# Gate and up projections by seven Strassen products, over pairs of inner chunks

## What is computed

```python
x = layernorm(x + attention(x))                  # 4 x 1024 tokens, width 512
def ffn(x):                                      # HIDDEN 512, INTER 2048
    x = fwht(x * SU_ug) / SCALE                  # Walsh-Hadamard, width 512
    x_up = x @ W_up.T * (Wscale_ug[:INTER] * SCALE)
    x_gate = x @ W_gate.T * (Wscale_ug[INTER:] * SCALE)
    x = silu(x_gate) * x_up
    x = fwht(x * SU_dp) / SCALE                  # width 2048
    return x @ W_down.T * (Wscale_dp * SCALE)
out = layernorm(x + ffn(x))
```

## Time and profile before

| | us |
|---|---|
| median of 3 runs | 1731.38 (1731.22 to 1732.57) |
| the profiled execution | 1730.56 |
| its span, first to last instruction | 1728.6 |
| TensorE busy in it | 1624.8 |
| VectorE busy | 922.0 |
| ScalarE busy | 654.6 |
| GpSimd busy | 365.9 |
| mean granted TensorE clock | 0.966 of full |

### The profile page before, as it was taken

The page is one execution under the profiler, slowest core; times in us unless marked ns, Lnnn a source line. Parts: engine busy times, 40 slices in busy tenths (PEclk is TensorE's granted clock), DMA queues, the critical chain, the costliest instruction groups (busy, mean ns, idle before and its releaser), DMA issues.

```text
span 1728.6 us, 22312 instructions
## 1 busy us (share of the span) xinstructions
PE 1624.8 (94%) x7848; PEld 1339.3 (77%) x7848; DVE 922.0 (53%) x1629; ACT 654.6 (38%) x1307; POOL 365.9 (21%) x518
## 2 busy tenths in 40 slices
PE   4989988998898869999999999999999999999997
PEld 2967777686686747778888888888888888888886
DVE  6765766576576644455445446446446445445444
ACT  3234225214313533334334334334334434434433
POOL 4372536336336300010010010020011001001000
PEclk8979998998998889999999999999999999999999
DMA  6040122113102071001001000000100100100000
GB/s 248 1 147 20 32 74 75 50 34 114 51 33 98 19 285 38 1 0 50 1 0 46 4 1 27 25 1 1 49 1 2 49 1 1 49 0 1 25 1 25
DMA packets 30622, 72.47 MB, mean 42 GB/s; under 512 B 2720, under 2 KB 3104, under 8 KB 29728
## 3 DMA queue, kind: packets, MB, share of 16 engines
q1 hardware_dynamic: 29488, 66.63, 10.9%
q10 hardware_dynamic: 1008, 4.20, 0.6%
HBM read 49.85 MB, written 20.97 MB: 41 GB/s over the span
## 4 chain that ended last, share of the span: by engine, by line
PE 63%; DMA 1%; DVE 0%; issue 0%; ACT 0%; SPq 0%; POOL 0%; POOLq 0%; DVEq 0%; ACTq 0%
PE ff_g_ps L87 7%; PE ff_g_ps L88 7%; PE ff_g_ps L89 7%; PE ff_acc L87 7%; PE ff_acc L89 7%; PE ff_acc L88 7%; PE ff_u_ps L89 7%; PE ff_u_ps L87 7%; PE ff_u_ps L88 7%; PE ff_w_ps L1496 1%; PE ff_x_ps L1482 1%; DMA ff_wd<-mixed_scratch 1%; PE ff_x_ps L1488 0%; PE ff_x_ps L1489 0%; DVE ff_bn L1467 0%
## 5 line engine op out<-in xcount | busy, mean ns | idle before, releaser
L1373 DVE TENSOR_TENSOR ff_gu_lo<-ff_wg,ff_gu_hi 128x512 fp32r<-128x512 f32 x128 | 91.0, 711 | 475.1 <-ACT ff_gu_hi L1282 475.1
L1298 ACT ACTIVATE ff_h_hi<-ff_hf 128x512 fp32r<-128x512 f32 x128 | 80.9, 632 | 352.2 <-DVE ff_hf L1382 352.2
L87 PE MATMUL ff_g_ps<-ff_x_hi,ff_gu_hi 128*128 128x512 f32 x512 | 206.2, 403 | 1.9 <-DVE ff_gu_lo L1374 1.1
L87 PE MATMUL ff_acc<-ff_d_hi,ff_h_hi 128*128 128x512 f32 x512 | 202.0, 395 | 0.0
L88 PE MATMUL ff_g_ps<-ff_x_lo,ff_gu_hi 128*128 128x512 f32 x512 | 200.2, 391 | 0.0
L89 PE MATMUL ff_g_ps<-ff_x_hi,ff_gu_lo 128*128 128x512 f32 x512 | 200.2, 391 | 0.0
L1289 ACT ACTIVATE ff_sg<-ff_g_ps,h_ug_scale 128x512 f32<-128x512 f32 x128 | 88.2, 689 | 294.7 <-PE ff_g_ps L89 294.7
L89 PE MATMUL ff_acc<-ff_d_hi,ff_h_lo 128*128 128x512 f32 x512 | 199.7, 390 | 0.0
L87 PE MATMUL ff_u_ps<-ff_x_hi,ff_gu_hi 128*128 128x512 f32 x512 | 199.4, 390 | 0.0
L88 PE MATMUL ff_u_ps<-ff_x_lo,ff_gu_hi 128*128 128x512 f32 x512 | 199.3, 389 | 0.0
L89 PE MATMUL ff_u_ps<-ff_x_hi,ff_gu_lo 128*128 128x512 f32 x512 | 199.3, 389 | 0.0
(11 more groups left out here) (295 smaller groups left out, 3213.1 us busy)
## 6 DMA issues: line engine op xcount, KB each, us to landing
at_xt<-in_xt SPq DMA_DIRECT2D x4, 2048.0 KB, 7.8
at_xn<-in_x SPq DMA_DIRECT2D x32, 256.0 KB, 2.8
x_scratch<-at_x SPq DMA_DIRECT2D x32, 256.0 KB, 2.0
at_wd_a<-in_wd SPq DMA_DIRECT2D x8, 512.0 KB, 4.1
mixed_scratch<-at_wd_a SPq DMA_DIRECT2D x8, 512.0 KB, 3.3
h_y<-x_scratch SPq DMA_DIRECT2D x4, 1024.0 KB, 5.6
ff_wg<-in_wg SPq DMA_DIRECT2D x4, 1024.0 KB, 14.1
ff_wu<-in_wu SPq DMA_DIRECT2D x4, 1024.0 KB, 14.3
```

Source lines behind the costliest of these rows:

```text
L87: pe.matmul(out, lhs_hi, rhs_hi, start=first, stop=False)
L1298: act.activation(h_hi[q][:, :], hf[q][:, :], ACT.Copy).then_inc(h_hi_s.sem, 1)
L1373: dve.tensor_tensor(gu_lo[q][:, 0, :, :], weight_chunk(wg, i), gu_hi[q][:, 0, :, :].bitcast(F32), ALU.subtract)
```

## The change

Two neighbouring chunks and the two halves of the 512 tokens (256 each), and the two halves of the width (256 each), make a 2 x 2 block product: weights A11, A12, A21, A22 (128 features by 256 of the width, gate and up side by side), tokens B11 to B22. One level of Strassen's scheme in Winograd's form needs seven block products in place of eight, and sums of blocks:

- Weight sums: GpSimd (`sum_weights`) S1 = A21 + A22, S2 = S1 - A11, A11 - A21, S4 = A12 - S2, once per pair, in the first block only. ScalarE rounds each of the 7 operands into a slot of a ring of 8 (`round_product`) and VectorE subtracts (`lower_product`), five products ahead of their use; SyncE stores each product's hi and lo (512 KB) in HBM (`store_product`). From the end of the first block on SyncE loads them from there (`load_product`): when product n has been used, its slot is filled with product n + 8. `wg` and `wu` are no longer kept.
- Token sums: GpSimd (`sum_tokens`) four per block. x_hi and x_lo hold 7 operands of 2 x 256 each and have one buffer.
- `multiply`: 12 matmuls of 256 tokens each (gate and up, two slices of the width, three passes). The seven products of a pair go to three banks, in the order a, b, c, b, a, b, c. Products 3 to 6 add onto what their bank holds, so each bank is read after each product: ScalarE copies product 0, VectorE adds five times (L1534, L1540, L1542, L1550, L1555), and the sums are the four outputs. `down` then has 24 matmuls for the pair before; d_hi and d_lo have one buffer of two chunks.

```diff
-        wg, wu = sb("wg", [P, DC, INTER]), sb("wu", [P, DC, INTER])
+        raw = [sb(f"raw{i}", [P, 4, 512]) for i in range(2)]
+        sums = sb("sums", [P, 3, 512])
+        ring = [sb(f"ring{i}", [P, 2, 2, 2, P], F32R) for i in range(RING)]
+        d_hi, d_lo = sb("d_hi", [P, 2, D], F32R), sb("d_lo", [P, 2, D], F32R)
+        x_hi, x_lo = sb("x_hi", [P, MULS, 2, HB2], F32R), sb("x_lo", [P, MULS, 2, HB2], F32R)
...
+        bank_a, bank_b, bank_c = ps("bank_a", [P, 2, HB2]), ps("bank_b", [P, 2, HB2]), ps("bank_c", [P, 2, HB2])
...
+        X_AT = {(4, 3): ("turn", 0), (4, 6): ("mix", 0), (4, 8): ("turn", 1), (5, 3): ("mix", 1), (5, 6): ("turn", 2),
+                (5, 8): ("mix", 2), (6, 3): ("turn", 3), (6, 6): ("mix", 3)}
...
+            def store_product(n):
+                sp.wait_ge(ring_lo, n + 1)
+                sp.dma_start(gu_dram[n], ring[n % RING][:, :, :, :, :].bitcast(F32)).then_inc(ring_in[n % RING].sem, 16)
+            def load_product(blk, n):
+                p, k = divmod(n, MULS)
+                sp.wait_ge(*mul_s.now(blk * PAIRS + p, k + 1))
...
+                ahead = n + RING
+                sp.dma_start(ring[n % RING][:, :, :, :, :].bitcast(F32), gu_dram[ahead % PRODUCTS]).then_inc(ring_in[n % RING].sem, 16)
...
+                for n in range(PRODUCTS):
+                    if n < PRODUCTS - RING or not last:
+                        load_product(blk, n)
+                    if n == MULS * 2 + 4:
+                        sp.wait_ge(*normed.last(blk, 1))
+                        sp.dma_start(out_dram[blk - 1], y[1 - parity][:, :, :]).then_inc(stored.sem, 16)
...
+            def round_product(n):
+                p, k = divmod(n, MULS)
+                if n >= RING:
+                    act.wait_ge(*mul_s.now((n - RING) // MULS, (n - RING) % MULS + 1))
+                    act.wait_ge(ring_in[n % RING].sem, 16 * (n // RING))
...
+                act.activation(both(n % RING, 0), operand(p, k), ACT.Copy).then_inc(ring_hi, 1)
+            def split_down(s, p, first):
+                act.wait_ge(down_s.sem, s)
...
+                for j in range(2):
+                    i = act.activation(by_piece(d_hi[:, j, :]), down_chunk(2 * p + j), ACT.Copy)
...
+                produce(0)
+                dve.wait_ge(*mul_s.now(s, 2))
+                dve.wait_ge(*m1_s.now(s, 1))
+                dve.tensor_tensor(c12[:, :, :], bank_b[:, :, :], c2[:, 0, :, :], ALU.add).then_inc(evict_s.sem, 1)
...
+            def multiply(s, blk, p, k, first):
+                n = MULS * p + k
+                r, bank = ring[n % RING], (bank_a, bank_b, bank_c, bank_b, bank_a, bank_b, bank_c)[k]
+                if first:
+                    pe.wait_ge(ring_lo, n + 1)
+                else:
+                    pe.wait_ge(*ring_in[n % RING].now(blk - 1, 16 * (n // RING + 1)))
...
+                for m in range(2):
+                    for c in range(2):
+                        for a, b in ((0, x_hi), (0, x_lo), (1, x_hi)):
+                            i = pe.matmul(bank[:, m, :], r[:, a, m, c, :], b[:, k, c, :], ...)
+                i.then_inc(mul_s.sem, 1)
...
+                for p in range(PAIRS):
+                    s = blk * PAIRS + p
+                    for k in range(MULS):
+                        multiply(s, blk, p, k, first)
+                        at(p, k)
...
+                    down(s - 1, (p - 1) % 2, p == 1, p == 0, False, lambda: at(p, 7))
+                    at(p, 8)
```

More of the change, by code:

```diff
@@ new lines, in butterfly @@
+                pool.tensor_tensor(m(2), m(4), m(6), ALU.subtract).then_inc(mixed.sem, 1)
+                pool.tensor_tensor(m(1), m(5), m(7), ALU.add).then_inc(mixed.sem, 1)
+                pool.tensor_tensor(m(3), m(5), m(7), ALU.subtract).then_inc(mixed.sem, 1)
+                pool.wait_ge(*mixed.now(blk, 8))
+                sum_tokens(blk, 8)
+            sum_weights(0)
+            pool.wait_ge(paired, 4)
+            pool.sem_inc(mixed.sem, 8)
+            sum_tokens(0, 8)
+            for p in range(1, PAIRS - 1):
+                sum_weights(p)
@@ L1332, in _, with at @@
+            def at(act, blk, p, pos, last):
+                if not last and (p, pos) in X_AT:
+                    what, c = X_AT[p, pos]
+                    (split_turned if what == "turn" else keep_mixed)(blk + 1, c)
+            def body(blk, idx, parity, first, last):
+                for p in range(PAIRS):
+                    step(blk * PAIRS + p, blk, p, parity, first, last)
+                if last:
+                    split_down(FBLK * PAIRS, PAIRS - 1, False)
             act.wait_ge(tab_in, 80)
@@ L1345, in _ @@
+            round_product(1)
+            for k in (0, 1, 2, 3, 4, 5, 6):
+                if k in (0, 4, 6):
+                    act.wait_ge(paired, 4 if k else 2)
+                else:
+                    act.wait_ge(*mixed.now(0, MIXED[k]))
+                act.activation(x_hi[:, k, :, :], tokens(k), ACT.Copy).then_inc(x_hi_s.sem, 1)
+                if k in (1, 3, 5):
+                    round_product(2 + k // 2)
             act.wait_ge(scaled, 3)
-            chunk_work(0, 0, 0, True)
@@ L1347, in _ @@
-            split_gu(1, 1, 1, True)
-            round_h(0, 0)
             blocks(act, body)
@@ new lines, in split_down, with product @@
+            def split_down(s, p):
+                dve.wait_ge(*d_hi_s.now(s - 1, 1))
+                for j in range(2):
+                    i = dve.tensor_tensor(by_piece(d_lo[:, j, :]), down_chunk(2 * p + j), by_piece(d_hi[:, j, :]).bitcast(F32), ALU.subtract)
+                i.then_inc(d_lo_s.sem, 1)
+            def product(s, p, n, j, up, gate, target):
+                dve.wait_ge(*silu_s.now(s, n + 1))
+                dve.scalar_tensor_tensor(target, up, ug_scale[:, 0, 2 * p + j:2 * p + j + 1], gate, ALU.mult, ALU.mult).then_inc(prod_s.sem, 1)
@@ L1431, in _ @@
+            def body(blk, idx, parity, first, last):
+                for p in range(PAIRS):
+                    step(blk * PAIRS + p, blk, idx, p, parity, first, last)
+                if last:
+                    split_down(FBLK * PAIRS, PAIRS - 1)
             dve.wait_ge(tab_in, 80)
@@ L1508, in down @@
-            def down(s, q, first, last, end=False):
-                pe.wait_ge(*h_lo_s.now(s, 1))
-                pe.wait_ge(*d_lo_s.now(s, 1))
-                for t in range(FT):
-                    k = slice(P * t, P * t + P)
-                    i = three_passes(pe, acc[:, t, :], h_hi[q][:, k], h_lo[q][:, k], d_hi[q][:, :], d_lo[q][:, :], first, last)
-                    if end:
-                        i.then_inc(end_down, 1)
+                pe.wait_ge(*xs_lo_s.now(1, turned))
+                pe.wait_ge(*xm_s.now(1, hadamarded))
@@ new lines, in down @@
+            def down(s, q, first, last, end=False, between=None):
+                pe.wait_ge(*h_lo_s.now(s, 2))
+                pe.wait_ge(*d_lo_s.now(s, 1))
+                for j in range(2):
+                    for t in range(FT):
+                        k = slice(P * t, P * t + P)
+                        i = three_passes(pe, acc[:, t, :], h_hi[q][:, j, k], h_lo[q][:, j, k], d_hi[:, j, :], d_lo[:, j, :], first and j == 0, last and j == 1)
+                        if end and j == 1:
+                            i.then_inc(end_down, 1)
+                    if j == 0 and between:
+                        between()
```

509 lines of the change are left out of this document (291 added, 218 removed).

## The result

The changed kernel takes 1699.67 us (median of 4 runs, 1698.63 to 1702.05), against 1731.3 for the kernel before measured beside it: a ratio of 0.982, 95% interval 0.981 to 0.984. It is 31.6 us faster; forecast were 81, and 1699.7 lies above the range of 1642 to 1680.

The account below looks back on a forecast made before the run. TensorE was taken as the bound, its time set by columns streamed: 1730.6 - 87.0 + 1.8 + 1.0 + 2.7 = 1649.1 us, given as 1650 since the median lies 0.8 above the profiled run; range 1642 to 1680.

Parts of the forecast that it names:

- What is removed, 84 x 0.1133: Gate/up per pair: 84 matmuls of 256 columns at 0.1133 us replace 48 of 512 at 0.2267, saving 87.0 us in all.
- The slow step, +1.8: Product streams with transposes or first-block `mix_down` inside may step at 0.1178 until the next down: 7.1 us at most, +1.8 taken.
- products at the slow step throughout: Rival: nothing in a 256-column product stream lets the 0.1178 step recover, +24 us instead of +1.8, 1672 us; chance 12%.
- The rival at 1699: Rival: the first matmul of each product takes 0.22 us in place of 0.11, 49 us more, 1699 us; chance 10%.
- Opening and first block, +1 (-5 to +10): Feed-forward opening and first block: 2.8 to 5 us gained, up to 10 lost to VectorE, raw weights and clock; +1 taken.
- the stream from HBM: Loading 29.4 MB of products per block, 255 GB/s with activations, was to cost TensorE nothing.
- its rival, 1923 and slower: Rival: HBM loads bind below 234 GB/s; at 194 GB/s a block takes 162 us, total 1923 us; chance 6%.
- the reads of the banks: VectorE's reads of the three banks between products: 0.6 us left at the thinnest, under 0.2 us per block, costed at nothing.
- the gap ahead of the last down: At the kernel's end, the last filling of d_hi and d_lo waits for the down before: +2.7 us, once.

## Why the prediction was wrong

- **What is removed, 84 x 0.1133: this step failed**, and it is most of the miss. The price was a row's, of the right shape and type, but from streams whose operands lay otherwise and which began otherwise. In the feed-forward half a matmul of 256 columns takes 0.1200, in the old kernel as in the new: 5376 x 0.0067 = 36 us. A pair saves 10.88 - 10.08 = 0.80 us, not 1.36, and the seven products 51 us instead of 87. "The trace shows no such fixed part between its two widths" was the sentence that misled: two widths from two places can hide a fixed part of 13.3 ns behind an advantage of 6.7. The Trainium skill, page "TensorE: Matmul & The Clock Gate", section "Back-to-back issue gap", which the prediction set beside the rows, had the sign right and a fifth of the size: by its 2.5 ns 11 of the 36 us would have been seen.
- **The slow step, +1.8.** It took every stream behind wide matmuls to start at the fast step and the transposes to slow it. In the change there is no fast step behind the wide matmuls, and the transposes don't slow anything, so the term is void; where they do change the step, with all tokens moved by 16, they make it shorter. The rival "products at the slow step throughout" was the nearest in mechanism, at 0.1178 and 1672; its size was short by 2.2 ns x 5376 = 12 us.
- **The rival at 1699** (each product's start lays its weight load bare) named the right time for a wrong reason: products follow each other at the same 0.120.
- **Opening and first block, +1 (-5 to +10).** What is not steady, execution less six blocks, was 1730.6 - 6 x 134.3 = 924.8. Two blocks' pairs at -1.36 x 8 and the terms +1 and +2.7 make 906.7 of it; it is 1699.25 - (1594.18 - 820.15) = 925.2. Of the 18.5 more, 2 x 672 x 0.0067 = 9.0 are steps. The other 9.5 are stops and clock. The first product started at 626.1 (forecast 626.6), but the fourth at 639.4 (636.2), as VectorE ran at 0.4 of its speed beside GpSimd; the trace then has stops of 2.0 us up to 653.1, 1.1 up to 738.1 and 2.0 up to 771.8, the last two waits for VectorE. The 49 steps at 1.2 GHz cost 49 x 0.093 = 4.6 us where the kernel before lost 12 x 0.2 = 2.4, so 2.2 of the 9.5 are the clock. The sum lies at the outer end of the bound given, 10.
- **The loop's branch back** was not in the sum: 3.9 + 1.1 = 5.0 us in the profiled execution, 1.6 of them at the lower clock.
- **Right**: the stream from HBM costs nothing (its rival, 1923 and slower, fell), the reads of the banks cost nothing in the steady blocks, and the gap ahead of the last down is 2.66 us against 2.7 (in the changed kernel's timeline, up to 1682.49).
- Together 36.0 - 1.8 + 9.5 + 5.0 = 48.7, against 1699.25 - 1649.1 = 50.2; six blocks at 128.2 and not 127.9 are the rest.

## To carry to other kernels

Before an algorithm that trades wide matmuls for more, narrower ones, measure the step of the narrow width in the kernel itself: here one edit of the kernel before, the same work in halves, gives the term that decides. Halving the columns did not halve the step, since here a matmul cost 13 ns beyond its columns and never less than 111 ns; a saving of one product in eight was worth 7% of the gate/up time and not 12.5%. A duration read from a row of the same shape still carries the place of its operands and what ran before it, by 10 ns at 0.12 us.
